# One set of statistics for two normalisations, and a reordered start, in an attention and MLP kernel

## The chip, the cores and the metric

The kernel is one program on one core of a Trainium2 chip. The metric is device time in microseconds (us), lower is better; the times given are those of single executions, and their median. The engines are TensorE (PE in the profile, PEld for its weight loads), VectorE (DVE), ScalarE (ACT), GpSimd (POOL) and SyncE (SP, which only issues transfers).

## The reference

```python
xn = layernorm(x)                      # x: (16, 512, 128), eps 1e-5
xn2 = layernorm(xn) * ln_g + ln_b      # inside the attention, a second time
q, k, v = (xn2 @ W + b for each)       # 16 heads of 8
content = (q + u_bias) @ k.T
pos = relative_shift((q + v_bias) @ (pe @ Wp).T)
attn = softmax((content + pos) / sqrt(8))
x = x + (attn @ v) @ Wo + bo + ffn(xn) # ffn: three layers of +-1 weights, relu between
```

All is float32. The relative shift moves row i of a head's 512x512 position scores by an amount that depends on i.

## The kernel before

**Batches, units and halves.** The kernel works through 16 batches. A batch has 16 heads; one head of one batch is a unit, and a unit has two halves, so a batch has 32 halves (h = 0 to 31 below, counted on over the batches). Each engine runs one loop over all halves and does its own share of each. TensorE computes position scores of a unit (L586, two 26x512 matmuls in most halves); ScalarE copies them to `pos_sb` (L394, L396); SyncE writes them to `shift` in HBM; ScalarE issues the load back with another pitch, which is the relative shift. It is issued 8 halves after the unit's first. Twelve halves after it, TensorE computes the content scores (L596), and VectorE adds the loaded position scores and takes the row extreme (L496), then subtracts it (L501). Seventeen halves after it, TensorE transposes the result (L605) into `ps_pt` and ScalarE takes the exponential (L404); TensorE multiplies with the values (L619).

**Jobs.** Everything else is a job, which TensorE does between these: T1 and TZ transpose the once and the twice normalised rows, QG, KG and PG (one for each of four groups of heads) compute queries, keys and the position table, V the values, L0, L1, L2 the layers of the MLP, TO, TH, WO, TY the output. Tuples `(half, name, group)` written out by hand (`START`, `FIRST`, `FIRST_NEXT`, `THIS`, `NEXT`, `LAST`) say in which half a job is done. All jobs write one PSUM bank, `ps_job`, and a job's first matmul waits until the job before has been copied out (L570, `wait(pe, s_jev, k - 1)`). ScalarE copies out all but V, TO, WO and TY, which VectorE takes (V at L441).

**Splits.** A matmul of full float32 precision is made of reduced ones: GpSimd splits what T1, L0, L1, QG, KG and PG gave into a high and a low part (`split`, L317 and L318 for the stacks `QS`, `KS`, `PS`; L326 and L327 for the MLP), from a ring of three buffers, `act_sb`.

**Normalisation.** `norm_stats(b, k)` on VectorE (L429, L432) takes mean and variance of `x` (k = 0) or of the once normalised `x1_sb` (k = 1), `norm(b, k)` on GpSimd raises the variance to the power -0.5 (L299, L300), and `scale_rows` (L237) writes `x1_sb` or `z_sb`; VectorE scales batch 0, GpSimd the others. Statistics for batch it + 2 stand in slots 6 and 8 of batch it (a slot is two halves), the scaling in slots 7 and 10. For batch 1 these slots fall before half 0, so each engine reaches them before its first half. The second statistics wait for the first scaling:

```python
else:
    dve.wait_ge(s_x1, b + 1)
```

**The start.** SyncE issues all loads. TensorE and ScalarE begin when all weights are there and VectorE has worked out three biases (`s_bias`, L469 to L475). Then come the jobs of `START` and the loop.

## Time and profile before

| | us |
|---|---|
| median of 3 runs | 1565.9 |
| lowest, highest | 1565.02, 1566.18 |
| the profiled execution | 1561.8 |
| its span, first to last instruction | 1560.0 |
| first position matmul (half 0) starts | 26.59 |
| half 12 (first content scores) starts | 62.89 |
| half 0 of batch 1 starts | 126.49 |
| one batch of the steady state | 92.5 |

Start times of halves are those of their first L586 matmul in the timeline. Busy shares over the span: TensorE 96%, VectorE 87%, ScalarE 80%, GpSimd 48%. DMA moves 353 GB/s in the mean; the highest of the page's 40 slices has 423. A row of the windows view has, after the stretch and its length in us, the busy time and number of instructions of PE, PEld, DVE, ACT and POOL, then the granted clock of TensorE, the DMA engines' busy share, and GB/s. A timeline row has start, duration, engine, line, operation, output<-input, sizes, and in brackets the idle time before it with what ended it. The page reads: busy time first, then the span in 40 slices, then the chain of work that ended last. A busy share is a mean over stages with different limits, so the stages have to be read one by one.

### The profile page before, as it was taken

What the parts mean: (1) busy time and instruction counts of PE and PEld (TensorE: products, weight loads), DVE (VectorE), ACT (ScalarE), POOL (GpSimd) and SP (SyncE); (2) the same over time, 40 slices, a digit from 0 to 9 for tenths busy, and PEclk for the clock granted to TensorE, in tenths of its full rate; (3) what the DMA queues carried; (4) which work ended last, traced back from release to release, by engine and by line L of the source; (5) the groups of instructions that cost most, each with busy time, mean ns of one, the idle gap of its engine ahead of it and who ended that gap; (6) DMA issues with size and microseconds to landing.
All of it is one profiled execution on the core that took longest, in us unless ns stands there. A gap on an engine that the chain in (4) does not pass through costs nothing.

```text
span 1560.0 us, 41383 instructions
## 1 busy us (share of the span) xinstructions
PE 1492.3 (96%) x16040; PEld 972.9 (62%) x16040; DVE 1350.5 (87%) x3593; ACT 1242.0 (80%) x1367; POOL 744.7 (48%) x743
## 2 busy tenths in 40 slices
PE   3989999999999999999999999999999999999997
PEld 1366666666666666666666666666666666666664
DVE  3278998989889898989989899898989989898895
ACT  1678888888888788878878888788888878887873
POOL 4864635445364554625455363554636455442300
PEclk9999999999999999999999999999999999999999
DMA  2799999999999999999999999999999999999992
GB/s 63 285 332 364 355 384 355 380 366 373 374 351 375 366 363 383 358 384 356 382 366 371 374 351 381 364 377 364 368 384 356 377 360 380 371 371 381 351 423 95
DMA packets 80435, 550.40 MB, mean 353 GB/s; under 512 B 9328, under 2 KB 10096, under 8 KB 14704
## 3 DMA queue, kind: packets, MB, share of 16 engines
q1 hardware_dynamic: 43376, 279.31, 48.2%
q10 hardware_dynamic: 36864, 268.45, 46.4%
q8 instruction: 128, 2.10, 0.5%
q14 instruction: 67, 0.55, 0.1%
HBM read 274.57 MB, written 273.15 MB: 351 GB/s over the span
## 4 chain that ended last, share of the span: by engine, by line
PE 72%; DVE 19%; issue 4%; ACT 4%; POOL 1%; DMA 0%; ACTq 0%; POOLq 0%; DVEq 0%
PE ps_pt L605 25%; PE ps_av L619 12%; PE ps_job L562 12%; PE ps_pos L586 10%; DVE sc_sb L496 8%; DVE sc_sb L501 7%; PE ps_job L523 4%; PE ps_job L526 3%; ACT pt_sb L404 3%; DVE stats L429 2%; PE ps_job L541 1%; PE ps_con L596 1%; PE ps_job L532 1%; PE ps_job L537 1%; DVE mv L432 1%
## 5 line engine op out<-in xcount | busy, mean ns | idle before, releaser
L496 DVE CUSTOM_DVE_ANT_0 sc_sb<-ps_con,sc_sb 128x512 f32<-128x512 f32 x1024 | 663.3, 684 | 155.2 <-PE ps_con L596 152.4
L394 ACT COPY pos_sb<-ps_pos 128x1024 f32<-128x1024 f32 x510 | 520.6, 1021 | 163.7 <-PE ps_pos L586 161.2
L501 DVE TENSOR_SCALAR sc_sb<-sc_sb,nmax 128x512 f32<-128x512 f32 x1024 | 604.7, 630 | 0.1
L605 PE MATMUL ps_pt<-c_sb,sc_sb 128*128 128x128 f32 x4096 | 560.4, 280 | 15.6 <-ACT pt_sb L404 8.5
L404 ACT ACTIVATE pt_sb<-ps_pt 128x1024 f32<-128x1024 f32 x512 | 526.4, 1028 | 45.5 <-PE ps_pt L605 44.9
L605 PEld LDWEIGHTS ps_pt<-c_sb,sc_sb 128*128 128x128 f32 x4096 | 441.6, 142 | 145.0 <-issue 79.9
L619 PE MATMUL ps_av<-pt_sb,v_sb 128*9 128x128 f32 x8192 | 320.7, 274 | 2.1 <-DVE o_sb L509 1.1
L619 PEld LDWEIGHTS ps_av<-pt_sb,v_sb 128*9 128x9 f32 x8192 | 173.0, 90 | 197.0 <-issue 192.9
L596 PE MATMUL ps_con<-k_stack,q_stack 26*128 26x512 f32 x1024 | 277.2, 497 | 14.6 <-DVE nmax L496 11.8
L586 PE MATMUL ps_pos<-p_stack,q_stack 26*128 26x512 f32 x1024 | 270.3, 504 | 0.8 <-POOLq L320 0.5
L326 POOL CAST h<-act_sb 128x512 fp32r<-128x512 f32 x128 | 80.3, 627 | 239.3 <-ACT act_sb L370 238.4
L317 POOL TENSOR_TENSOR q_stack<-act_sb,c_sb 128x512 fp32r<-128x512 f32 x64 | 66.9, 1046 | 240.1 <-ACT act_sb L367 239.7
L586 PEld LDWEIGHTS ps_pos<-p_stack,q_stack 26*128 26x128 f32 x1024 | 100.8, 184 | 127.2 <-issue 112.8
L562 PE MATMUL ps_job<-h,w 128*128 128x512 f32 x640 | 173.6, 410 | 0.6 <-ACT act_sb L370 0.3
L327 POOL TENSOR_TENSOR h<-act_sb,h 128x512 fp32r<-128x512 f32 x128 | 166.5, 1301 | 10.3
L317 POOL TENSOR_TENSOR k_stack<-act_sb,c_sb 128x512 fp32r<-128x512 f32 x64 | 67.4, 1053 | 170.1 <-ACT act_sb L367 169.9
L370 ACT ACTIVATE act_sb<-ps_job,col 128x512 f32<-128x512 f32 x128 | 88.8, 694 | 59.8 <-PE ps_job L562 59.7
L562 PEld LDWEIGHTS ps_job<-h,w 128*128 128x128 f32 x640 | 114.6, 191 | 24.4 <-DVE heads L449 3.7
L596 PEld LDWEIGHTS ps_con<-k_stack,q_stack 26*128 26x128 f32 x1024 | 104.2, 182 | 32.6 <-DVE nmax L496 30.6
L318 POOL TENSOR_TENSOR q_stack<-act_sb,q_stack 128x512 fp32r<-128x512 f32 x64 | 82.3, 1286 | 5.0
L318 POOL TENSOR_TENSOR k_stack<-act_sb,k_stack 128x512 fp32r<-128x512 f32 x64 | 82.1, 1283 | 5.0
L496 DVE DVE_READ_ACCUMULATOR2_ANT nmax<- 128x1 f32 x1024 | 83.4, 81 | 0.0
(70 smaller groups left out, 969.8 us busy)
## 6 DMA issues: line engine op xcount, KB each, us to landing
...
x_sb<-in_x SPq DMA_DIRECT2D x16, 256.0 KB, 9.5
out<-x_sb SPq DMA_DIRECT2D x16, 256.0 KB, 10.9
...
o_t<-in_wp SPq DMA_DIRECT2D x1, 256.0 KB, 5.7
heads<-in_pe_t SPq DMA_DIRECT2D x1, 256.0 KB, 6.9
```

What stands on the lines that cost most here:

```text
L317: own(pool.tensor_tensor(dst, src, low.broadcast_to([P, S]), ALU.mult))
L318: pool.tensor_tensor(dst, src, dst.bitcast(F32), ALU.subtract).then_inc(s_hl, 1)
L327: pool.tensor_tensor(dst[:, 1, :], src, dst[:, 0, :].bitcast(F32), ALU.subtract) \
L394: act.copy(to, ps_pos[:, :, :]).then_inc(s_pe, 1)
L404: act.activation(pt_sb[:, 2 * i:2 * i + 2, :], ps_pt[:, :, :], ACT.Exp, scale=-1.0) \
L496: dve.tensor_tensor_reduce(sc_sb[:, m % N_SC, t, :], ps_con[:, k, :], sc_sb[:, m % N_SC, t, :], -SCALE, 3.4e38, ALU.add, ALU.min, nmax[:, ...
L501: dve.tensor_scalar(sc_sb[:, m % N_SC, t, :], sc_sb[:, m % N_SC, t, :], nmax[:, m % N_SC, t:t + 1], None, ALU.subtract).then_inc(s_sub, 1)
L562: return pe.matmul(ps_job[:, :], lhs, src[:, a, hl, :], start=(a == 0 and hl == 0), stop=(a == len(before) - 1 and hl == 1))
L586: ins = pe.matmul(ps_pos[:, bank, :], QS[rows, g, t * P:(t + 1) * P], PS[rows, g, :], start=True, stop=True)
L596: pe.matmul(ps_con[:, bank, :], QS[rows, g, t * P:(t + 1) * P], KS[rows, g, :], start=True, stop=True).then_inc(s_con, 1)
L605: last = pe.transpose(ps_pt[:, j % 2, t * P:(t + 1) * P], sc_sb[:, u % N_SC, t, j * P:(j + 1) * P], id_sb)
L619: last = pe.matmul(ps_av[32 * t:32 * t + DH + 1, h % 4, :], v_sb[:, b % 2, j, h, :], pt_sb[:, j, t * P:(t + 1) * P], start=(j == 0), stop= ...
```

## The change

1. **One set of statistics.** The second normalisation scales `x` with the first one's mean, and its factor comes from the same variance v: (v (1 + eps) + eps^2)^-0.5 in place of the statistics of `x1_sb`. `norm_stats(b)` runs once for each batch (slot 6), `scales(b)` on GpSimd makes both factors at once: two small operations and one power over 8 columns. The scalings stay in slots 7 and 10.
2. **Batches 0 and 1.** VectorE takes the statistics of batch 1 in half 1 and does both its scalings in half 6, GpSimd its factors in half 2. Of batch 0, `z_sb` is scaled first, `x1_sb` later.
3. **Own banks.** The seven jobs of the new `START` (TZ, PG 0, QG 0, KG 0, PG 1, PG 2, PG 3) write banks of `ps_pt`, `ps_con` and `ps_job` that are not yet in use (`BANK`), and don't wait for the job before. QG, KG and PG among them are copied to free score buffers (`RAW`) instead of the ring. VectorE splits PG 0 to 3 and QG 0, GpSimd KG 0.
4. **Waits and loads.** ScalarE issues the loads of `consts`, `wp` and `pe`, SyncE the others. A small ScalarE activation at the start brings its table load forward. TensorE waits for `consts` alone before TZ, and for each bias where it is used; the bias for `wp` is made first.
5. **The order of batch 0's jobs.** PG 1, PG 2 and PG 3 leave halves 2, 5 and 11. V moves from half 0 to 2, L0 from halves 6, 8, 9, 10 to 4, 6, 8, 10, and L1 from 13, 14, 18, 19 to 12 to 15. Halves 18 and 19 have no job any more.

The names in the rows below: `z_sb` and `x1_sb` are the normalised rows (TZ, T1), `z_q` and `z_t` the transposed ones (QG; KG and V), `heads`/`o_t` hold the position encoding and its weights at the start (PG), `w0`, `w1`, `w2` the MLP weights. TensorE from its first matmul on, before:

```order
L549 MATMUL ps_job<-c_sb,z_sb 128x128 x4
L523 MATMUL ps_job<-z_q,stack_w_sb 128x512
L529 MATMUL ps_job<-heads,o_t 128x512
L526 MATMUL ps_job<-z_t,stack_w_sb 128x512
L586 MATMUL ps_pos<-p_stack,q_stack 128x512
L549 MATMUL ps_job<-c_sb,x1_sb 128x128 x4
L537 MATMUL ps_job<-c_sb,z_t 128x128 x4
L586 MATMUL ps_pos<-p_stack,q_stack 128x512
L523 MATMUL ps_job<-z_q,stack_w_sb 128x512
L586 MATMUL ps_pos<-p_stack,q_stack 128x512 x2
L529 MATMUL ps_job<-heads,o_t 128x512
```

and after:

```order
L613 MATMUL ps_pt<-c_sb,z_sb 128x128 x4
L593 MATMUL ps_con<-heads,o_t 128x512
L587 MATMUL ps_pt<-z_q,stack_w_sb 128x512
L590 MATMUL ps_job<-z_t,stack_w_sb 128x512
L593 MATMUL ps_con<-heads,o_t 128x512 x3
L662 MATMUL ps_pos<-p_stack,q_stack 128x512
L613 MATMUL ps_job<-c_sb,x1_sb 128x128 x4
L662 MATMUL ps_pos<-p_stack,q_stack 128x512
L587 MATMUL ps_job<-z_q,stack_w_sb 128x512
```

The PG matmuls now stand ahead of the first `ps_pos` matmul, and half 0 has lost V. VectorE between the MLP weights and its first values, before:

```order
L483 TENSOR_SCALAR w1<-pt_sb 128x2048
L484 TENSOR_SCALAR w2<-pt_sb 128x512
L429 BN_STATS stats<-x_sb 128x6 x4
L432 BN_AGGR mv<-stats 128x2 x4
L429 BN_STATS stats<-x1_sb 128x6 x4
L432 BN_AGGR mv<-stats 128x2 x4
L441 TENSOR_TENSOR v_sb<-ps_job,c_sb 128x64x8
```

and after, from the last split of the position table on:

```order
L482 TENSOR_TENSOR p_stack<-sc_sb,c_sb 128x512
L483 TENSOR_TENSOR p_stack<-sc_sb,p_stack 128x512
L538 TENSOR_SCALAR w0<-pt_sb 128x512
L539 TENSOR_SCALAR y_t<-pt_sb 128x512
L540 TENSOR_TENSOR w0<-w0,y_t 128x512
L541 TENSOR_SCALAR w1<-pt_sb 128x2048
L542 TENSOR_SCALAR w2<-pt_sb 128x512
L475 BN_STATS stats<-x_sb 128x6 x4
L478 BN_AGGR mv<-stats 128x2 x4
L491 TENSOR_TENSOR v_sb<-ps_job,c_sb 128x64x8
L251 TENSOR_SCALAR x1_sb<-x_sb,mv,rstd 128x128 x4
L251 TENSOR_SCALAR z_sb<-x_sb,mv,rstd 128x128 x4
```

The second statistics, which read what GpSimd scaled, are gone from the place ahead of `v_sb`, and the scaling of batch 1 stands behind it. The diff, cut to its core:

```diff
-        START = ((0, "TZ", 0), (1, "QG", 0), (2, "PG", 0), (3, "KG", 0))
...
+        START = ((0, "TZ", 0), (1, "PG", 0), (2, "QG", 0), (3, "KG", 0), (4, "PG", 1), (5, "PG", 2), (6, "PG", 3))
...
+        BANK = {("TZ", 0, 0): ps_pt[:, 0, :], ("QG", 0, 0): ps_pt[:, 1, :], ("PG", 0, 0): ps_con[:, 0, :],
+                ("PG", 0, 1): ps_con[:, 1, :], ("PG", 0, 2): ps_con[:, 0, :], ("PG", 0, 3): ps_con[:, 1, :],
+                ("KG", 0, 0): ps_job[:, :]}
...
-        STATS_SLOTS, NORM_SLOTS = (6, 8), (7, 10)
...
+            return [b if 0 <= b < B and slot == k else None for k in (6, 7, 10)]
...
+            def scales(b):
+                pool.wait_ge(s_st, b + 1)
+                own(pool.tensor_scalar(var_eps[:, 0, :], mv[:, :, 1], EPS, None, ALU.add))
+                own(pool.tensor_scalar(var_eps[:, 1, :], mv[:, :, 1], 1.0 + EPS, EPS * EPS, ALU.mult, ALU.add))
+                own(pool.tensor_tensor(rstd[:, :, :].rearrange("p k t -> p (k t)"),
+                                       var_eps[:, :, :].rearrange("p k t -> p (k t)"), half_pow[:, :], ALU.pow))
...
+                _, first, second = slot_of(h // 2)
+                if h % 2 == 0 and first is not None:
+                    scales(first)
+                    norm(first, 0)
+                if h % 2 == 0 and second is not None:
+                    norm(second, 1)
...
-            act.wait_ge(s_w, 64)
+            act.dma_start(c_sb[:, :], consts).then_inc(s_c, 16)
+            act.dma_start(wp_sb[:, :], wp).then_inc(s_w, 16)
+            act.dma_start(pe_sb[:, :], pe_t).then_inc(s_w, 16)
             act.wait_ge(s_ones, ONES)
...
+            norm_stats(0)
+            dve.wait_ge(s_rstd, 1)
+            scale_rows(dve, 0, 1)
+            dve.wait_ge(s_c, 16)
+            dve.wait_ge(s_w, 48)
...
+            dve.wait_ge(s_jev, job("PG", 0, 0))
+            stack(PS[:, 0, :], RAW[("PG", 0, 0)], LOW_K, s_ps)
+            dve.wait_ge(s_jev, job("QG", 0, 0))
+            stack(QS[:, 0, :], RAW[("QG", 0, 0)], LOW_Q, s_qs)
+            scale_rows(dve, 0, 0)
+            for c in range(1, GROUPS):
+                dve.wait_ge(s_jev, job("PG", 0, c))
+                stack(PS[:, c, :], RAW[("PG", 0, c)], LOW_K, s_ps)
...
+                if h == 1:
+                    norm_stats(1)
+                if h == 6:
+                    dve.wait_ge(s_rstd, 2)
+                    dve.wait_ge(s_job, job("T1", 0))
+                    scale_rows(dve, 1, 0)
+                    scale_rows(dve, 1, 1)
...
+                if part == 0 and (name, b, c) in BANK:
+                    if name in ("QG", "PG") and c < 2:
+                        pe.wait_ge(s_w, 48)
+                    if name == "PG":
+                        pe.wait_ge(s_bias, 1)
+                        if c >= 2:
+                            pe.wait_ge(s_jev, job("PG", 0, c - 2))
+                    if name == "QG":
+                        pe.wait_ge(s_jev, job("TZ", 0))
+                    if name == "KG":
+                        pe.wait_ge(s_bias, 2)
+                        pe.wait_ge(s_zt, 1)
```

ScalarE copies out `z_q` right after TZ, then PG 0, then QG 0, and only then makes `z_t`, which sets `s_zt`.

## Rows read from the trace of the kernel before

**Rows 1.** Windows of batch 0's first 20 halves: busy time of each engine, clock, DMA.
```profile
26.59:37.98 11.39, 6.61 (x16) 3.53 (x17) 1.83 (x9) 1.95 (x4) 9.05 (x12) 1.00 0.00 0
37.98:62.89 24.91, 24.48 (x42) 7.86 (x42) 0.00 (x0) 16.80 (x20) 23.07 (x23) 1.00 0.56 211
62.89:74.84 11.95, 11.23 (x35) 5.67 (x35) 7.92 (x25) 6.53 (x8) 9.57 (x11) 1.00 1.02 381
74.84:92.62 17.78, 14.27 (x97) 9.65 (x96) 11.76 (x34) 11.18 (x13) 12.06 (x13) 0.90 0.82 321
```

**Rows 2.** The same view for two whole batches of the steady state.
```profile
404.28:498.20 93.92, 92.21 (x1006) 60.95 (x1003) 84.34 (x223) 77.20 (x86) 46.47 (x46) 0.98 0.99 363
498.20:590.70 92.50, 90.73 (x1006) 59.88 (x1003) 84.19 (x223) 77.20 (x86) 46.68 (x46) 1.00 1.00 368
```

**Rows 3.** Windows: half 14 and halves 16 to 21, batch 6, then batch 14.
```profile
631.79:635.58 3.79, 2.99 (x33) 1.74 (x29) 3.75 (x16) 2.04 (x3) 2.97 (x4) 1.00 1.00 409
638.71:655.28 16.57, 16.27 (x188) 10.50 (x184) 15.96 (x46) 15.63 (x19) 10.99 (x11) 1.00 1.01 344
1373.53:1376.15 2.62, 2.51 (x33) 1.57 (x29) 2.62 (x9) 2.05 (x3) 0.00 (x0) 1.00 0.98 397
1379.28:1395.82 16.54, 15.81 (x189) 10.32 (x185) 15.83 (x38) 15.59 (x19) 8.74 (x8) 1.00 1.02 391
```

**Rows 4.** Waits, 26 to 36 us: engine and line waited for; total, times, longest.
```profile
DVE stats L429 <- POOL x_sb L237: 16.0, 1, 16.0
...
PE ps_job L523 <- DVE v_sb L441: 4.1, 1, 4.1
```

**Rows 5.** The same view, 76 to 90 us.
```profile
DVE stats L429 <- POOL x_sb L237: 2.2, 1, 2.2
```

**Rows 6.** Timeline from the start: start us, us, engine, line, work [idle before].
```profile
3.83 0.87 DVE L429 BATCH_NORM_STATS2 stats<-x_sb 128x6 f32<-128x128 f32 x4 [2.44 <-DMA x_sb<-in_x]
...
5.53 1.04 POOL L300 TENSOR_TENSOR rstd<-var_eps,half_pow 128x4 f32<-128x4 f32 x1
...
10.62 1.11 DVE L237 TENSOR_SCALAR z_sb<-x_sb,mv,rstd 128x128 f32<-128x128 f32 x4 [1.53 <-POOLq L302]
...
12.46 0.28 DVE L469 TENSOR_TENSOR biased<-o_t,c_sb 128x128 f32<-128x128 f32 x1
...
13.92 1.08 PE L549 MATMUL ps_job<-c_sb,z_sb 128*128 128x128 f32 x4 [13.92 <-DVE col L476]
...
15.11 1.28 ACT L361 ACT_TABLE_LOAD   x1 [15.11 <-PE ps_job L549]
...
17.08 1.25 ACT L362 ACTIVATE z_t<-ps_job,c_sb 128x512 f32<-128x512 f32 x1
...
20.50 0.69 ACT L367 ACTIVATE act_sb<-ps_job,c_sb 128x512 f32<-128x512 f32 x1 [2.17 <-PE ps_job L523]
...
21.23 2.08 PE L529 MATMUL ps_job<-heads,o_t 128*128 128x512 f32 x2 [0.78 <-ACT act_sb L367]
```

**Rows 7.** DMA issues: size, microseconds from issue to landing.
```profile
heads<-in_pe_t SPq DMA_DIRECT2D x1, 256.0 KB, 6.9
```

**Rows 8.** Timeline of later halves of batch 0, TensorE and GpSimd.
```profile
44.43 2.07 PE L523 MATMUL ps_job<-z_q,stack_w_sb 128*128 128x512 f32 x2
44.45 1.04 POOL L317 TENSOR_TENSOR p_stack<-act_sb,c_sb 128x512 fp32r<-128x512 f32 x1 [0.18 <-ACT act_sb L367]
...
47.00 1.04 POOL L317 TENSOR_TENSOR k_stack<-act_sb,c_sb 128x512 fp32r<-128x512 f32 x1 [0.18 <-POOL p_stack L318]
...
56.88 1.22 PE L562 MATMUL ps_job<-x_t,w 128*128 128x512 f32 x2
```

**Rows 9.** Timeline, where the matmuls get faster.
```profile
66.48 3.63 PE L562 MATMUL ps_job<-h,w 128*128 128x512 f32 x8
...
70.89 2.12 PE L562 MATMUL ps_job<-h,w 128*128 128x512 f32 x8 [0.34 <-ACT act_sb L370]
...
73.78 1.12 PE L526 MATMUL ps_job<-z_t,stack_w_sb 128*128 128x512 f32 x2 [0.34 <-ACT act_sb L370]
```

More of the change, by code:

```diff
@@ L124, in attention_mlp @@
         ps_job = psum("ps_job", [P, S])
+        s_c = sem("s_c")
         s_w = sem("s_w")
@@ L310, in split @@
                 pool.wait_ge(s_jev, job(name, b, c))
-                if name in ("QG", "KG", "PG"):
-                    dst, low, ready = {"QG": (QS, LOW_Q, s_qs), "KG": (KS, LOW_K, s_ks),
-                                       "PG": (PS, LOW_K, s_ps)}[name]
+                if name in ("QG", "KG"):
+                    dst, low, ready = {"QG": (QS, LOW_Q, s_qs), "KG": (KS, LOW_K, s_ks)}[name]
                     dst = dst[:, c, :]
+                    if b == 0 and c == 1 and name == "QG":
+                        pool.wait_ge(s_qs, 1)
                     if b > 0:
@@ L534, in block @@
                     def block(t):
-                        dst, cut = ps_job[:, t * P:(t + 1) * P], slice(t * P, (t + 1) * P)
+                        dst, cut = out[:, t * P:(t + 1) * P], slice(t * P, (t + 1) * P)
                         if name == "V":
```

141 lines of the change are left out of this document (79 added, 62 removed).

## The prediction, made before the changed kernel was run

> **What bounds the kernel now.** I read the chain of waits first: it lies mostly on TensorE, then on VectorE. Such a share mixes stages, so next come the start times of the halves in the timeline, and then the windows and the waits of the stretches that stick out.
>
> The steady state repeats itself to a few hundredths: a batch takes 92.5 us, and two batches take 1.42 longer (93.92); in those the granted clock is 0.98 in place of 1.00 [rows 2]. Batch 0 is different. From the first position matmul (26.59) to batch 1 it takes 99.9 (126.49 - 26.59), 7.4 more than a steady one, and 26.59 go by before it. Three things stand out. Its halves 0 and 1 take 11.39, with TensorE busy for 6.61 of them [rows 1]. VectorE waits there 16.0 us for GpSimd's scaling of batch 1, because the second statistics need it; V of batch 0 stands behind that wait, `ps_job` stays full, and TensorE waits 4.1 [rows 4]. Later, in halves 16 to 19 (17.78 for work of which TensorE does 14.27), VectorE waits 2.2 for the same reason, behind GpSimd's queue of splits, and the clock is at 0.90 [rows 1, 5]. Third, the start: TZ begins only at 13.92, when VectorE has finished the last bias, though `z_sb` was ready at 11.7 [rows 6].
>
> **Statistics, in the steady state: nothing.** The change takes one block of about 1.2 us off VectorE in each batch. VectorE is busy 84 of 92.5 us, so it looks as if this could give 1.2 in each of 14 batches. The trace has its own test of this: batch 14 has neither block, since no batch 16 follows. The first block (slot 6) costs TensorE 3.79 - 2.62 = 1.17 us in half 14; this block stays. Around the second (slot 8), halves 16 to 21 take 16.57 with it and 16.54 without, since ScalarE is busy for 15.6 of them either way [rows 3]. So I take 0.0 for the block that goes, between 0 and a gain of 0.03 a batch. On GpSimd slot 10 loses a small operation and a power of about 1.04, slot 7 gains one small operation and four more columns of power. No row shows a power over 8 columns. The one over 4 takes 1.04, as long as a product over 512 [rows 6, 8], so the price hardly goes by columns; bounds are 0 and another 1.04. I take 0, and the upper bound is a rival below.
>
> **The start: 2.1 us earlier.** x has landed at 3.83, the power starts at 5.53 and takes 1.04 [rows 6]. One more small GpSimd step costs less than the power; estimate 0.3. So the scaling of `z_sb` (1.11) starts at 5.53 + 0.3 + 1.13 = 7.0 in place of 10.62 and ends at 8.1. TZ (1.08) follows, to 9.3; the 1.28 of the table load has left the path, since ScalarE does it while it waits for x [rows 6]. PG 0 needs the position table's loads and the first bias. The last of these loads took 6.9 us from issue [rows 7]; issued third on ScalarE, 1 to 3 us in, it lands at 8 to 10. The bias took at most 1.5 (12.46 to 13.92, with what follows it) [rows 6]. PG 0 starts between 9.3 and 10.8; I take 9.9. Then PG 0 and QG 0, 2.08 each, to 14.1. Now a wait that the change adds: ScalarE copies QG 0 (0.7) before it makes `z_t` (1.25), and KG 0 waits for `z_t`, with PG 1 to 3 queued behind it on TensorE: 16.1. Four matmul jobs of 2.08 without a pause give 24.4, and the first position matmul starts at 24.5 in place of 26.59. **Term: -2.1**, bounds -2.7 and -1.1. VectorE's splits of PG 0 and QG 0 are done by 17, well before; GpSimd's of KG 0 is needed only in half 12.
>
> On the loads, the trace shows that SyncE issues them one after the other and that the last lands 6.9 after its issue. The Trainium skill (DMA: Bandwidth & Descriptors, Issuing engines are not separate DMA queues) says that two issuing engines share the same 16 DMA engines, and that only the time of issuing is saved. By that rule the split of the issues alone gives about an issue or two, and x can land a little later since it now shares the engines with `consts`; with PG 0 at 10.8 the term would be -1.2.
>
> **Halves 0 to 11: 6.5 us less.** Now 11.39 + 24.91 = 36.30 [rows 1]. A half with QG, KG or PG takes its matmuls, 2.07, and 0.78 until ScalarE has emptied the bank: 2.85. One with L0 takes 1.22 + 0.78 = 2.0 [rows 6, 8]. After: half 0 with T1 alone 1.8, half 1 (QG) 2.8, half 2 (V) 2.9, five with KG or QG 14.25, four with L0 8.0, sum 29.8. **Term: -6.5.** V now waits for VectorE's MLP weights and the statistics of batch 1, which end at about 31 while V's matmuls end at 32; the cover is 1 us, and beyond it each us costs one. GpSimd has 6 stacks of 2.55 (44.45 to 47.00) [rows 8], 5 other splits of about 2 and the factors of batch 1 (1.7): 27.0 in 29.8 us. It just keeps up. Bounds: -6.9 and -5.
>
> **Halves 12 to 15: 1.7 us more.** Now 11.95 [rows 1]. They get all four L1. One costs 3.63 + 0.78 = 4.4 where the matmuls speed up in its midst, 2.12 + 0.78 = 2.9 after it [rows 9]. 4.4 + 3 x 2.9 = 13.1; if the clock rises one half later, 14.4. I take 13.7. **Term: +1.7**, bounds +1.2 and +2.4.
>
> **Halves 16 to 19: 8.0 us less.** Now 17.78 [rows 1]. L1 2 and 3 are gone from 18 and 19, VectorE's wait (2.2) [rows 5] is gone, and with it the fall of the clock that followed TensorE's stall. What remains is TZ's two copies and the ordinary work: per half, VectorE and ScalarE have about 2.4, with TZ near 2.8. 9.8 together, bounds 9.2 and 11.6. **Term: -8.0**, bounds -8.6 and -6.2. What is late next is GpSimd: its scaling of batch 2 waits for T1 of batch 1, which is in half 16, with the split of L1 3 and of T1 queued behind. I have that split done 1.5 us before L0 of half 20 asks for it.
>
> The other twelve halves keep their jobs, and so do all batches from 1 on: 0.
>
> **The sum.** -2.1 - 6.5 + 1.7 - 8.0 = -14.9. Against the profiled execution that is a span of 1560.0 - 14.9 = 1545.1 and a time of 1561.8 - 14.9 = 1546.9. The median of the runs is 4.1 above the profiled execution, and the start of a program doesn't depend on that, so from the median: 1565.9 - 14.9 = **1551.0**. The bounds of the terms add up to -18.2 and -9.9; two or none of the clock's falls in the steady state, or two more, shift it by 2.8 either way. The likeliest case alone: 1547 to 1555.
>
> **Rivals.**
>
> *The clock rises in the start.* The matmuls of L1 get from 3.63 to 2.12 for eight, those of a stack from 2.07 to 1.12 [rows 8, 9], though the granted clock reads 1.00 throughout [rows 1]: these are the two levels, 1.2 and 2.4 GHz. It rose inside eight matmuls without a pause, not in the 25 us of alternating position matmuls and jobs before. The new start has 8.3 us of jobs without a pause. If they raise it, PG 2 and 3 give 2.1, halves 0 to 11 fall to GpSimd's 27.0 (2.8 less), and L1 0 gives 1.5: 6.4 more, 1544.6. Against it: the matmuls of QG and PG filled some 70% of those 25 us and raised nothing. The Trainium skill (TensorE: Matmul & The Clock Gate, What's actually happening) says that the low rate is the default and that activity releases it, which would speak for this rival.
>
> *Part of the gain is given back in batch 0.* Two mechanisms: GpSimd's queue at half 20 runs out of its 1.5 us, or V waits for VectorE; or the transfers bind, since halves of 2.4 ask for 2 x 1.05 MB in 4.8 us, 437 GB/s, where halves 12 to 15 moved 381 [rows 1]. Each gives back 2 to 5 us, together up to 6: 1555 to 1557.
>
> *Slower: GpSimd's slot 7.* If the power over 8 columns costs another 1.04 and the small step 0.3, the split of QG 3, which waits behind the scaling, comes late in each of 14 batches, the ring fills and ScalarE and TensorE wait. At 1.34 a batch that is 18.8 us against 14.9: 1554.9 if half of it shows, 1569.8 if all. It decides from 1.1 us a batch on. Against it: GpSimd is busy for only 46.7 of 92.5 us [rows 2].
>
> *The change doesn't do what it says*, because a new wait keeps TensorE from starting before 26 and halves 18 and 19 stay long: a gain under 3.1, 1564.
>
> **Chances.** The forecast 0.56, the early clock 0.18, given back 0.19, no difference 0.03, slower 0.04. The range takes in the early clock and nearly all of the given-back case: 1543.5 to 1557.5. About 0.2%, 3.1 us, is what a measurement can tell here: faster 0.93, same 0.03, slower 0.04.
>
> **What would show it.** TZ at 8 to 9 us; the first position matmul at 24.5 (26 or more: the start's term is wrong); half 12 at 54.3; batch 1 at 111.6 in place of 126.49; a batch of 92.5 as before, with half 14 still at 3.8; TensorE's matmuls of 2.07 until half 12. The prediction is wrong if batches become shorter than 92.3 (then the second statistics did cost something) or longer than 92.7 (GpSimd), or if halves 0 to 11 take more than 32.

## The result, and the profile after

The changed kernel takes 1550.3 us in the median of 4 runs (1547.8 to 1553.57), the kernel before beside it 1566.04 (1565.02 to 1566.75). The ratio is 0.9901, with a 95% interval of 0.9879 to 0.9923: faster by 1.0%. The prediction was 1551.0, so the number is right. The working behind it is right only in part: two of its steps failed in opposite directions.

The page of the profiled execution (1551.94 us), its first line and the 40 slices of granted clock:

```profile
span 1550.1 us, 41206 instructions
...
PEclk8799999999999999999999999999999999999999
```

In the clock row the second slice (39 to 78 us) is at 0.7. The windows view over the first 20 halves answers [rows 1]: halves 0 and 1, 2 to 11, 12 to 15, 16 to 19. The fifth row is half 3 alone, the sixth halves 4 to 11, the last a batch of the steady state, for [rows 2].

```profile
21.39:24.52 3.13, 2.64 (x9) 1.08 (x9) 3.10 (x4) 2.15 (x4) 1.66 (x3) 1.00 0.00 0
24.52:55.01 30.49, 23.05 (x47) 8.12 (x46) 12.62 (x24) 16.21 (x19) 22.82 (x22) 0.58 0.51 180
55.01:68.30 13.29, 12.40 (x49) 7.73 (x48) 8.83 (x25) 6.63 (x8) 8.88 (x9) 0.81 0.97 363
68.30:78.91 10.61, 8.27 (x83) 5.39 (x82) 10.00 (x26) 9.58 (x11) 9.77 (x11) 0.91 1.01 381
26.46:35.60 9.14, 2.50 (x5) 0.68 (x5) 6.97 (x16) 1.01 (x1) 4.50 (x5) 0.66 0.29 116
35.60:55.01 19.41, 18.96 (x33) 6.28 (x32) 3.74 (x8) 13.60 (x16) 16.38 (x16) 0.50 0.66 228
112.82:205.46 92.64, 90.40 (x1006) 59.66 (x1002) 84.14 (x215) 77.23 (x86) 46.22 (x45) 1.00 1.00 365
```

The two long halves of the kernel before are gone (11.39 became 3.13). In their place stands half 3 with 9.14 us, in which TensorE works for 2.50. From then to half 12 its clock is at 0.50.

| | before | predicted | after |
|---|---|---|---|
| first position matmul (half 0) | 26.59 | 24.5 | 21.39 |
| halves 0 to 11 take | 36.30 | 29.8 | 33.62 |
| half 12 starts | 62.89 | 54.3 | 55.01 |
| halves 12 to 15 take | 11.95 | 13.7 | 13.29 |
| halves 16 to 19 take | 17.78 | 9.8 | 10.61 |
| half 0 of batch 1 starts | 126.49 | 111.6 | 112.82 |
| most batches of the steady state | 92.5 | 92.5 | 92.62 |

Of the gain 13.67 us are there when batch 1 begins. Batches 1 to 14 give back 0.7, the last batch 1.5 and what follows it 1.6; the spans differ by 9.9 (1560.0 to 1550.1). The last batch and what follows it vary between executions of the same code: they take 88.66 and 50.7 here, 86.66 to 87.94 and 49.1 to 51.9 in the experiment kernels, 87.16 and 49.1 before. The single profiled executions stand differently to their medians, 4.2 below it before and 1.6 above it after. That is why the medians differ by 15.7. How much of the 5.8 beyond the spans' 9.9 is the change's stays open.

**The start.** The timeline of the changed kernel up to half 0, for [rows 6]:

```profile
4.64 0.87 DVE L475 BATCH_NORM_STATS2 stats<-x_sb 128x6 f32<-128x128 f32 x4 [3.25 <-DMA x_sb<-in_x]
...
6.62 1.67 POOL L313 TENSOR_TENSOR rstd<-var_eps,half_pow 128x8 f32<-128x8 f32 x1
...
9.63 1.09 PE L613 MATMUL ps_pt<-c_sb,z_sb 128*128 128x128 f32 x4 [9.63 <-DVE z_sb L251]
...
10.51 1.98 PE L593 MATMUL ps_con<-heads,o_t 128*128 128x512 f32 x2
...
16.23 2.04 PE L590 MATMUL ps_job<-z_t,stack_w_sb 128*128 128x512 f32 x2 [2.03 <-ACT z_t L396]
...
18.06 3.39 PE L593 MATMUL ps_con<-heads,o_t 128*128 128x512 f32 x6
...
21.39 0.50 PE L662 MATMUL ps_pos<-p_stack,q_stack 26*128 26x512 f32 x1
```

TZ starts 1.4 us later than forecast: x is there 0.81 later, and the power over 8 columns takes 0.63 more. KG 0 still starts at 16.23 (forecast 16.1). PG 0 follows right behind TZ at 10.51, 0.6 after the forecast 9.9, and it and QG 0 take 3.7 together in place of 4.2. An earlier TZ would have helped little: in e8 below, with TZ 1.05 earlier, PG 0 starts 0.35 earlier and waits for its bias. Then comes the surprise: six PG matmuls take 3.39 in place of 6.2, and the first position matmul has 0.50 where it has 0.79 at the low rate. TensorE has gone to 2.4 GHz in these matmuls, near 19 us; in the kernel before it did so in the last of the eight matmuls from 66.48 on [rows 9], some 50 us later. (Ahead of the first rise the views give a granted clock of 1.00, though the matmuls run at the low rate, so the start is read from the matmuls.)

**Half 3.** Waits of the changed kernel between 24 and 36 us, for [rows 4], and VectorE's timeline there:

```profile
ACT act_sb L414 <- PE ps_job L590: 7.7, 1, 7.7
...
PE ps_job L590 <- DVE v_sb L491: 6.6, 1, 6.6
```

```profile
25.01 1.64 DVE L483 TENSOR_TENSOR p_stack<-sc_sb,p_stack 128x512 fp32r<-128x512 f32 x1
26.58 1.26 DVE L538 TENSOR_SCALAR w<-pt_sb 128x512 fp32r<-128x512 uint8 x1
27.76 1.48 DVE L539 TENSOR_SCALAR y_t<-pt_sb 128x512 f32<-128x512 uint8 x1
29.27 0.69 DVE L540 TENSOR_TENSOR w<-w,y_t 128x512 fp32r<-128x512 f32 x1
29.88 1.22 DVE L541 TENSOR_SCALAR w<-pt_sb 128x2048 fp32r<-128x2048 uint8 x1
...
31.68 0.87 DVE L475 BATCH_NORM_STATS2 stats<-x_sb 128x6 f32<-128x128 f32 x4 [0.25 <-DVE w L542]
32.59 0.38 DVE L478 BATCH_NORM_AGGREGATE mv<-stats 128x2 f32<-128x6 f32 x4
32.88 0.66 DVE L491 TENSOR_TENSOR v_sb<-ps_job,c_sb 128x512 f32<-128x512 f32 x1
```

V's matmuls end at 26.5, and VectorE empties their bank at 32.88, after its MLP weights and statistics. TensorE stands idle for 6.6 us, more than the 5.2 that it gained in the start, and after that its clock is low again.

### The profile page after: what moved, and what is told of

Its sections match the earlier page's. It is cut to its first block, busy times and chain, and to the rows that moved or that the text cites. A ratio compares the mean times of both kernels' runs of the same rounds, so it can differ in the third digit from the quotient of the medians.

```text
span 1550.1 us, 41206 instructions
## 1 busy us (share of the span) xinstructions
PE 1483.5 (96%) x16040; PEld 968.8 (62%) x16040; DVE 1360.5 (88%) x3483; ACT 1241.5 (80%) x1368; POOL 722.2 (47%) x709
## 4 chain that ended last, share of the span: by engine, by line
PE 75%; DVE 14%; ACT 5%; issue 3%; DMA 3%; ACTq 0%; POOL 0%; DVEq 0%; POOLq 0%
PE ps_pt L681 26%; PE ps_av L695 13%; PE ps_job L626 12%; PE ps_pos L662 10%; DVE sc_sb L559 5%; DVE sc_sb L564 5%; PE ps_job L590 4%; PE ps_job L587 4%; ACT pt_sb L453 3%; DMA sc_sb<-shift 2%; ACT z_t L409 1%; PE ps_con L672 1%; PE ps_job L605 1%; PE ps_job L596 1%; DVE stats L475 1%
## 5 line engine op out<-in xcount | busy, mean ns | idle before, releaser
L564 DVE TENSOR_SCALAR sc_sb<-sc_sb,nmax 128x512 f32<-128x512 f32 x1024 | 617.5, 643 | 0.1
L672 PE MATMUL ps_con<-k_stack,q_stack 26*128 26x512 f32 x1024 | 273.0, 497 | 12.2 <-DVE nmax L559 10.3
L346 POOL TENSOR_TENSOR h<-act_sb,h 128x512 fp32r<-128x512 f32 x128 | 170.4, 1331 | 10.3
```

The lines of the kernel that those rows point to most:

```text
L346: pool.tensor_tensor(dst[:, 1, :], src, dst[:, 0, :].bitcast(F32), ALU.subtract) \
L564: dve.tensor_scalar(sc_sb[:, m % N_SC, t, :], sc_sb[:, m % N_SC, t, :], nmax[:, m % N_SC, t:t + 1], None, ALU.subtract).then_inc(s_sub, 1)
L672: pe.matmul(ps_con[:, bank, :], QS[rows, g, t * P:(t + 1) * P], KS[rows, g, :], start=True, stop=True).then_inc(s_con, 1)
```

## The experiments

Each kernel ran beside the kernel before on the same chip. That one took 1566.04 us beside the changed kernel, but 1562.35 to 1564.25 beside the others, so times are to be compared by the last column; the expectations below speak of times for 1566. The table gives the starts of halves in the profiled executions, and the runs' times. In each of these executions two to four of the batches 1 to 14 take 93.8 to 94.0 us in place of 92.6, at a lower granted clock (the first of [rows 2] is one), so a difference of 1 or 2 us between two kernels says little.

| kernel | half 0 | half 12 | half 20 | batch 1 | median (lowest to highest) | ratio to before (95%) |
|---|---|---|---|---|---|---|
| before | 26.59 | 62.89 | 92.62 | 126.49 | | |
| changed | 21.39 | 55.01 | 78.91 | 112.82 | 1550.3 (1547.8 to 1553.57) | 0.9901 (0.9879 to 0.9923) |
| e1_stats_alone | 24.66 | 57.95 | 83.69 | 116.87 | 1553.31 (1551.66 to 1554.59) | 0.9926 (0.9910 to 0.9943) |
| e2_second_block | 21.48 | 54.08 | 76.92 | 110.83 | 1550.38 (1548.14 to 1551.28) | 0.9908 (0.9893 to 0.9923) |
| e3_v_first | 21.10 | 47.26 | 73.00 | 106.87 | 1543.93 (1540.92 to 1546.0) | 0.9867 (0.9852 to 0.9882) |
| e4_one_bank | 28.97 | 59.76 | 82.40 | 115.80 | 1554.84 (1553.83 to 1556.24) | 0.9939 (0.9924 to 0.9954) |
| e5_sync_loads | 20.14 | 54.03 | 77.12 | 110.51 | 1549.1 (1547.29 to 1552.4) | 0.9915 (0.9897 to 0.9934) |
| e6_more_splits | 21.41 | 42.54 | 67.64 | 101.00 | 1542.94 (1537.62 to 1545.94) | 0.9873 (0.9842 to 0.9904) |
| e7_gpsimd_splits | 22.75 | 51.94 | 74.93 | 108.34 | 1548.63 (1546.53 to 1550.14) | 0.9909 (0.9892 to 0.9925) |
| e8_power4 | 22.39 | 54.95 | 77.94 | 111.29 | 1548.41 (1546.63 to 1549.32) | 0.9900 (0.9878 to 0.9921) |
| e9_v_first_again | 21.34 | 47.46 | 73.22 | 107.03 | 1541.69 (1538.62 to 1542.47) | 0.9852 (0.9825 to 0.9878) |
| e10_more_splits_again | 21.45 | 42.56 | 67.69 | 101.08 | 1539.71 (1538.21 to 1544.5) | 0.9851 (0.9825 to 0.9876) |
| e11_all | 21.59 | 42.67 | 69.16 | 103.54 | 1541.81 (1541.11 to 1543.6) | 0.9861 (0.9839 to 0.9882) |
| e12_two_powers | 23.43 | 55.76 | 79.96 | 115.53 | 1551.0 (1549.03 to 1556.47) | 0.9909 (0.9875 to 0.9943) |

### e1_stats_alone: one part of the change by itself

The kernel before, with one set of statistics and nothing else of the change:

```diff
-        STATS_SLOTS, NORM_SLOTS = (6, 8), (7, 10)
+        STATS_SLOTS, NORM_SLOTS = (6,), (7, 10)
...
-                if k == 0:
-                    dve.wait_ge(s_x[b % N_X], 16 * (b // N_X + 1))
...
-                else:
-                    dve.wait_ge(s_x1, b + 1)
```

> The kernel before with one set of statistics and nothing else of the change: the jobs, banks, splits and loads are those of before. Theory: the statistics are most of the gain, since both waits of VectorE for GpSimd's scaling go with them, and the second one's wait also took the clock down. Start: the second statistics and power leave VectorE's path, 1.9 us less, the first position matmul near 24.7. Half 1 falls from 6.91 to about 2.9, halves 18 and 19 from 13.0 to about 6.5. Sum 12 less: 1554. Rival: only the two waits seen in the waits view are won, 4.1 + 2.2, so 1559.7. A steady batch should be 92.5 by both.

Batch 1 begins at 116.87, which is 9.6 of the 13.7 us. Half 1 falls from 6.91 to 2.86, and V no longer waits for GpSimd. The time is the theory's: 0.9926 of 1566 is 1554.5, forecast 1554. Windows of halves 0 and 1, and of 16 to 19:

```profile
24.66:32.01 7.35, 6.61 (x17) 3.54 (x17) 0.69 (x1) 1.96 (x4) 6.52 (x8) 1.00 0.00 0
...
69.72:83.69 13.97, 12.69 (x98) 8.34 (x98) 11.20 (x28) 10.93 (x13) 13.12 (x14) 1.00 1.01 396
```

Read beside [rows 1] (11.39 and 17.78), these rows show what the wait cost: 4.0 us in halves 0 and 1 (the first row), where TensorE's work is the same 6.61, and 3.8 in halves 16 to 19. There TensorE is busy for 12.69 in place of 14.27, because the clock, 0.90 before, stays up: part of the 3.8 is the clock that the stall had taken. Another 1.9 are in the start, where second statistics and a second power no longer stand between the scalings of `x1_sb` and `z_sb`. Seven tenths of the change's gain at batch 1 come from the single set of statistics, not from the starts that its diff spends most lines on.

### e2_second_block: the removed work, put back without its dependence

The changed kernel, and VectorE takes a second, unused set of statistics of `x` in slot 8:

```diff
+                    for t in range(NT):
+                        last = dve.bn_stats(stats_b[:, t, :], x_sb[:, extra % N_X][:, t, :])
+                    own(last)
+                    for t in range(NT):
+                        last = dve.bn_aggr(mv_b[:, t, :], stats_b[:, t, :])
```

> The changed kernel with a second block of statistics put back on VectorE in slot 8 of each batch, as long as the one removed (1.25 us), from x and unused, so that it waits for nothing. Theory: ScalarE bounds halves 16 to 21, the block costs nothing in the steady state: a batch stays at 92.6 and the time at 1550 (within 2). Rival: VectorE's 1.25 us count in each of 14 batches: a batch of 93.8, 1567.

```profile
110.83:203.43 92.60, 90.71 (x1008) 60.04 (x1004) 84.29 (x223) 77.26 (x86) 45.99 (x45) 1.00 0.99 364
```

VectorE has its 223 instructions again as in [rows 2], and the batch takes 92.60 as without them. The work itself was all but free, as the prediction read from [rows 3]. The batch hides two differences of 0.1, though. Half 21 takes 2.95 to 2.97 in batches 1 to 13, which have the block, and 2.85 in batch 14, which has none; in the changed kernel it takes 2.86. And halves 2, 5, 8 and 10, which have the L1 jobs, take 15.71 together as before and 15.81 in the changed kernel. The L1 job of half 10 of batch 3, before, changed and here:

```profile
343.26 2.07 PE L562 MATMUL ps_job<-h,w 128*128 128x512 f32 x8
...
329.78 2.12 PE L626 MATMUL ps_job<-h,w 128*128 128x512 f32 x8
...
327.68 2.07 PE L636 MATMUL ps_job<-h,w 128*128 128x512 f32 x8
```

The block stands only in slot 8 of batches 0 to 13. So this run shows that in halves 16 to 19 e1's gain is the dependence. In halves 0 and 1 the waits [rows 4] say the same, and the 1.9 of the start are work on the path, which this run doesn't put back.

### e3_v_first: what V's wait costs

```diff
-            dve.wait_ge(s_wb, 48)
-            half0 = y_t[:, :]
...
-                if h == 1:
-                    norm_stats(1)
...
+                if h == 2:
+                    first_weights()
+                    norm_stats(1)
+                    other_weights()
```

VectorE now takes V out before it makes the MLP weights and the statistics of batch 1 (GpSimd's factors move from half 2 to 4).

> The changed kernel with V of batch 0 taken by VectorE ahead of the MLP weights and of the statistics of batch 1, which follow it in half 2 (GpSimd's factors then in half 4). In the changed kernel TensorE waits 6.6 us for V's copy in half 3. Theory: the early position matmuls (21.4) only ran into that wait, and it is VectorE's queue that holds half 12 at 55.0. With V first, half 3 falls from 9.14 to below 3.5 and half 12 comes at 49 to 51, so about 5 less: 1545.5. Rival: L0 of half 4, which needs the MLP weights, inherits the wait; then half 4 grows by 3 or more and the gain is 1 to 2: 1549.

```profile
26.28 0.69 DVE L491 TENSOR_TENSOR v_sb<-ps_job,c_sb 128x512 f32<-128x512 f32 x1 [1.63 <-PE ps_job L606]
```

```profile
27.03 1.12 PE L595 MATMUL ps_job<-z_t,stack_w_sb 128*128 128x512 f32 x2 [0.35 <-DVE v_sb L491]
...
40.40 2.07 PE L592 MATMUL ps_job<-z_q,stack_w_sb 128*128 128x512 f32 x2 [2.52 <-ACT act_sb L419]
```

Half 3 takes 1.91 in place of 9.14, half 12 starts 7.8 us earlier, and the time falls to 0.9867 of before, 5 us better than the changed kernel. Beyond its 6.6 us the wait had cost the clock: without it the stacks run at 1.12 us a pair until half 8, and halves 4 to 8 take 9.3 in place of 11.7. Then the next limit shows, the waits of e3 between 40 and 48 us:

```profile
PE ps_job L592 <- ACT act_sb L419: 2.5, 1, 2.5
ACT act_sb L419 <- POOL q_stack L337: 2.3, 1, 2.3
```

ScalarE finds no free buffer in the ring because GpSimd is behind, TensorE stands for 2.5 us, and the clock falls again (2.07 for the pair). Half 9 takes 5.02 in place of 2.85, so nearly all that the clock had given is gone again.

### e4_one_bank: the start's jobs in one bank

```diff
-        BANK = {("TZ", 0, 0): ps_pt[:, 0, :], ("QG", 0, 0): ps_pt[:, 1, :], ("PG", 0, 0): ps_con[:, 0, :],
+        BANK = {j: ps_job[:, :] for j in (("TZ", 0, 0), ("QG", 0, 0), ("PG", 0, 0), ("PG", 0, 1), ("PG", 0, 2),
...
-                if part == 0 and (name, b, c) not in BANK:
+                if part == 0:
```

> The changed kernel with all seven jobs of the start in the one bank of before, each waiting until the job before has been copied out; order, splits and loads stay. Theory: each job then takes 2.85 in place of 2.08, z_t is made before PG 0, the first position matmul starts at 29 to 30 and not at 21.4; the jobs are no longer without a pause, so the matmuls stay at 2.08 and don't speed up before half 12. Of the 8 us the wait for V eats most: half 12 comes at 59 to 60 in place of 55.0, 1554.8. Rival: the start counts in full, 8 more: 1558.5.

```profile
21.47 2.08 PE L591 MATMUL ps_job<-heads,o_t 128*128 128x512 f32 x2 [0.78 <-ACT sc_sb L395]
...
26.96 2.07 PE L591 MATMUL ps_job<-heads,o_t 128*128 128x512 f32 x2 [0.67 <-ACT sc_sb L390]
28.97 0.79 PE L655 MATMUL ps_pos<-p_stack,q_stack 26*128 26x512 f32 x1
```

With 0.7 us of pause between them the jobs stay at the low rate, and half 0 starts 7.6 us later. Yet batch 1 starts only 3.0 us later than in the changed kernel (5.0 later than in e2): V's matmuls now end when VectorE is nearly ready (half 3 takes 3.99). So 2.6 to 4.6 of the 7.6 us that own banks gain in the start have ended in V's wait or behind it by then. The median is the forecast 1554.8 as it stands; by its ratio it is 1556.5, between the theory's 1554.8 and the rival's 1558.5, and the interval is too wide (2.4 us either way) to choose. Halves and batch 1 speak for the theory.

### e5_sync_loads: the loads from one engine

```diff
+            sp.dma_start(c_sb[:, :], consts).then_inc(s_c, 16)
...
-            act.dma_start(c_sb[:, :], consts).then_inc(s_c, 16)
-            act.dma_start(wp_sb[:, :], wp).then_inc(s_w, 16)
-            act.dma_start(pe_sb[:, :], pe_t).then_inc(s_w, 16)
```

> The changed kernel, but SyncE issues all loads again, in the old order (x, consts, the stacked weights, wp, pe, then the rest). It prices the loads from two engines alone. In the changed kernel x_sb is there at 4.64 us, 0.81 later than before (3.83), and PG 0 starts at 10.51 right behind its predecessors. Theory: x arrives alone again, near 3.85, so TZ starts about 0.8 earlier than 9.63; but pe and wp are issued behind three other loads and PG 0 waits for them until 11 to 12, so half 0 starts at 21.4 to 22.4 in place of 21.39, and the median is 1550.3 to 1551.3, nothing that can be told from the changed kernel. Rival: the issuing engine matters more than that, and the last load that PG 0 needs lands at 13 or later; then half 0 starts at 24 or later and the time is 1553 or more.

```profile
8.85 1.09 PE L613 MATMUL ps_pt<-c_sb,z_sb 128*128 128x128 f32 x4 [8.85 <-DVE z_sb L251]
...
10.60 2.05 PE L593 MATMUL ps_con<-heads,o_t 128*128 128x512 f32 x2 [0.66 <-DVE o_t L522]
...
16.39 1.10 PE L590 MATMUL ps_job<-z_t,stack_w_sb 128*128 128x512 f32 x2 [2.04 <-ACT z_t L396]
17.32 2.88 PE L593 MATMUL ps_con<-heads,o_t 128*128 128x512 f32 x6
```

x lands 0.79 earlier, the position table's loads later, and PG 0 starts at 10.60 in place of 10.51: issuing from two engines is worth 0.1 us here. In e8 below, where PG 0 waits for its bias as it does here, two engines have it start at 10.16, 0.44 earlier. Half 0 nonetheless starts 1.25 earlier, which I had not expected: the clock rose already for KG 0 (1.10). The times can't be told from those of the changed kernel. The Trainium skill (DMA: Bandwidth & Descriptors, Issuing engines are not separate DMA queues) says that only time of issuing is saved; this trace agrees, by 0.1 us (0.44 against e8's, where the last of these loads is issued 1.4 us earlier).

### e6_more_splits: GpSimd relieved

e3_v_first, and VectorE also splits QG 2 and QG 3 of batch 0:

```diff
+                    if j in (("QG", 0, 2), ("QG", 0, 3)):
+                        dve.wait_ge(s_jev, job(*j))
+                        dve.wait_ge(s_qs, j[2])
+                        stack(QS[:, j[2], :], RAW[j], LOW_Q, s_qs)
```

> The kernel of e3_v_first, and VectorE also splits QG 2 and QG 3 of batch 0, which takes two of GpSimd's stacks (2.55 us each) off its queue. In e3 half 9 took 5.02 us, since ScalarE waited 2.3 for a free buffer of GpSimd's ring, TensorE stood idle for 2.5 and its clock fell again, so that L1 0 and L1 1 took 4.72 and 4.56. Theory: GpSimd is the next limit there; without those two stacks half 9 takes 2.0 to 2.9, the clock stays up, half 12 starts at 43 to 45 in place of 47.26, L1 takes 2.9, half 16 starts at 55 to 58 in place of 62.38, and the time is 1538 to 1541. Rival: the transfers bind (halves of 2.0 to 2.4 us ask for 1.05 MB each 2 of them, over 430 GB/s, where the page never shows more than 423): then halves 12 to 16 wait for sc_sb from the DMA, half 20 starts within 1 us of e3's 106.87 - 33.9 = 73.0, and the time is 1543 to 1545.

```profile
21.41:42.54 21.13, 16.85 (x55) 6.58 (x54) 16.97 (x26) 17.67 (x23) 16.72 (x16) 1.00 0.52 188
42.54:57.83 15.29, 12.63 (x47) 7.49 (x46) 13.45 (x31) 6.58 (x8) 12.79 (x12) 0.89 1.02 394
```

Half 9 takes 1.64 in place of 5.02, halves 0 to 11 take 21.13 us at a granted clock of 1.00, and half 12 starts at 42.54. The transfers don't bind: half 20 starts at 67.64, where the rival had 73.0. What is late next is L1 0 (half 12 takes 5.00): its matmuls wait for GpSimd's splits of L0, 1.62 us in the longest case, and the clock falls once more. Batch 1 starts 5.9 us before e3's, but the time misses the forecast of 1538 to 1541: 0.9873 of 1566 is 1546, no better than e3's 0.9867. The two were on different chips; e9 and e10 ask again.

### e7_gpsimd_splits: VectorE's splits undone

```diff
-                    if (name, b, c) == ("KG", 0, 0):
-                        pool.wait_ge(s_jev, job("KG", 0))
-                        stack(KS[:, 0, :], RAW[("KG", 0, 0)], LOW_K, s_ks)
+                    if (name, b, c) in RAW:
...
+                        stack(dst[:, c, :], RAW[(name, b, c)], low, ready)
```

> The changed kernel, but GpSimd does all six of the start's splits; VectorE's five (PG 0 to 3, QG 0) go to it, in the order of the jobs. It is the part 'VectorE splits five of them' undone alone. Five stacks of 2.55 us are 12.8 us more on GpSimd. Theory: the first position matmul, which needs PG 0 and QG 0, moves little (its TensorE work ends at 21.4 anyway), V no longer waits 6.6 us for VectorE (its matmuls' bank is emptied at 27 to 28), but GpSimd runs behind from half 1 on: QG 1's split comes at 31 or later and ScalarE waits for the ring; half 12 starts at 56 to 60 in place of 55.01 and the time is 1552 to 1556. Rival: GpSimd catches up while TensorE is at its low rate, and with V's wait gone half 12 starts at 49 to 52; then the time is 1545 to 1548 and the split on VectorE was of no use.

```profile
28.67 1.13 PE L585 MATMUL ps_job<-z_t,stack_w_sb 128*128 128x512 f32 x2 [0.35 <-DVE v_sb L493]
...
32.19 1.06 PE L621 MATMUL ps_job<-x_t,w 128*128 128x512 f32 x2 [1.96 <-POOL x_t L346]
```

V's wait is gone and halves 4 and 7 wait for GpSimd in its place (3.45 and 4.20 in place of 2.00 and 2.86). Half 12 starts at 51.94, as the rival had it (49 to 52). Batch 1 starts at 108.34, 4.5 us before the changed kernel's, of which two more slow batches take 3.0 back in this execution. The time is the changed kernel's (0.9909; of 1566 that is 1552, at the lower end of my forecast of 1552 to 1556, not the rival's 1545 to 1548). In this form of the start, moving five stacks to VectorE moved the queue rather than shortening it.

This kernel also prices an overlap. VectorE's first weights run here while GpSimd is idle, the later ones beside its split:

```profile
12.42 0.42 DVE L533 TENSOR_SCALAR w<-pt_sb 128x512 fp32r<-128x512 uint8 x1
...
13.27 1.53 POOL L321 TENSOR_TENSOR p_stack<-sc_sb,c_sb 128x512 fp32r<-128x512 f32 x1 [4.98 <-ACT sc_sb L390]
13.82 2.06 DVE L536 TENSOR_SCALAR w<-pt_sb 128x2048 fp32r<-128x2048 uint8 x1
14.88 2.15 POOL L322 TENSOR_TENSOR p_stack<-sc_sb,p_stack 128x512 fp32r<-128x512 f32 x1
15.81 1.51 DVE L537 TENSOR_SCALAR w<-pt_sb 128x512 fp32r<-128x512 uint8 x1
```

The same 128x512 conversion takes 0.42 alone and 1.51 beside GpSimd, and GpSimd's split 1.53 and 2.15 where it takes 1.04 and 1.28 alone. The Trainium skill (SBUF — State Buffer, Who interferes with whom) says that a `tensor_scalar` in a two-port mode takes a port pair that VectorE shares with GpSimd, that whoever comes second stands still for it, and that a `tensor_tensor` with two SBUF inputs contends with GpSimd's reads. The rows fit: both sides get longer, and in the changed kernel a `p_stack` operation takes 1.64 in place of 0.69. In which mode this conversion runs they don't show.

### e8_power4: the first power over four columns

```diff
+            own(pool.tensor_scalar(var_eps[:, 1, :], mv[:, :, 1], 1.0 + EPS, EPS * EPS, ALU.mult, ALU.add))
+            own(pool.tensor_tensor(rstd[:, 1, :], var_eps[:, 1, :], half_pow[:, 0:NT], ALU.pow))
+            pool.sem_inc(s_rstd, 1)
```

> The changed kernel, but for batch 0 GpSimd works out the factor of the second normalisation first and alone: one small operation and a power over 4 columns, and the other factor behind it. In the changed kernel the power over 8 columns takes 1.67 us, the one over 4 in the kernel before took 1.04. Theory: the power's price goes up with its columns, 1.04 here again (0.16 per column beyond some 0.4), and with the small operation of 0.32 that leaves the path TZ starts at 8.65 to 8.7 in place of 9.63. PG 0 then waits for its bias or its loads and starts at 9.6 to 10.1 in place of 10.51; half 0 starts at 20.5 to 21.0 in place of 21.39. V's wait in half 3 grows by what the start gained, since VectorE's queue sets its end, so half 12 moves by less than 0.5 and the time is 1549.5 to 1550.3, not to be told from the changed kernel. Rival: the 1.67 is what any power takes behind two operations of GpSimd's in a row; then TZ is at 9.3 and nothing else moves.

```profile
6.19 1.04 POOL L351 TENSOR_TENSOR rstd<-var_eps,half_pow 128x4 f32<-128x4 f32 x1
...
8.58 1.09 PE L619 MATMUL ps_pt<-c_sb,z_sb 128*128 128x128 f32 x4 [8.58 <-DVE z_sb L251]
...
10.16 2.05 PE L599 MATMUL ps_con<-heads,o_t 128*128 128x512 f32 x2 [0.49 <-DVE o_t L527]
...
17.77 4.69 PE L599 MATMUL ps_con<-heads,o_t 128*128 128x512 f32 x6
```

The power's price goes with its columns (1.04 for 4, 1.67 for 8), and TZ starts where expected. PG 0 gains 0.35, and half 0 starts 1.0 *later*: the same six matmuls take 4.69, because the clock rose later in them. An earlier start was paid back by the clock. The time is that of the changed kernel.

### e9_v_first_again and e10_more_splits_again: the two side by side

> The kernel of e3_v_first once more, in one call with e10 and e11, because the two were timed on different chips so far (ratios 0.9867 and 0.9873). Theory: e10's batch 0 ends 5.9 us earlier (half 0 of batch 1 at 101.0, here at 106.87) and about 5 of it must be in the time: this kernel at 0.9867, e10 at 0.9830 to 0.9845 of the kernel before. Rival: the clock gives it back; executions of e10 that are not profiled fall to the low rate for longer (their mean clocks were 0.983, 0.986 and 0.996 beside 0.991 in the profiled one, the times 1545.2, 1545.9 and 1537.6), and then the two are within 1.5 us of each other, each with a wide spread that goes with the clock.

> The kernel of e6_more_splits once more. Theory: 1537.6 to 1541 in most executions, the one at 1545 an exception. Rival: its executions fall into two groups by the clock, near 1538 at a mean clock of 0.996 and near 1545 at 0.985, because in some of them the clock falls again in batch 0 and stays low for a long stretch; then the median is about 1542.5.

The profiled executions repeat to 0.2 us (batch 1 at 107.03 and 101.08). Spans are 1540.6 and 1536.4, so 4.2 of the 5.9 us are still there at the end; the rest lies in what follows the last batch, 49.1 against 50.8. But the medians are 1541.69 and 1539.71, and the ratios 0.9852 and 0.9851, each with 0.25% either way. So e9's theory, 5 us in the time, failed, and the ratios are its rival's. Of e10's own two, the theory held: three of four executions lie at 1538.2 to 1540.3 and one at 1544.5, and not in the rival's two groups by clock. The executions with the lower clock are the longer ones on the whole (e10: 1538.21 at 0.993, 1544.5 at 0.990), not without exception (1540.25 at 0.990). How much of e6's 5.9 us an execution keeps is open; both kernels beat the one before and the changed one.

### e11_all: e6, e5 and e8 together

> All that helped, together: e6_more_splits, the loads from SyncE in the old order (in e5_sync_loads half 0 started at 20.14 in place of 21.39), and the first power over 4 columns (e8_power4). Theory: TZ starts at 7.9, half 0 at 19.8 to 20.3, half 12 at 41 to 42, half 0 of batch 1 at 99 to 100, and the time is 1 to 2 us under e10. Rival: in some executions the clock falls in batch 0 and takes back more than that; then it can't be told from e10.

```profile
17.22 4.43 PE L611 MATMUL ps_con<-heads,o_t 128*128 128x512 f32 x6
```

TZ starts at 7.90 as expected, but PG 0 waits for its loads (10.67), and the clock rises for KG 0 (1.10 us) and is low again within the next six matmuls: half 0 at 21.59 (forecast 19.8 to 20.3). L1 of halves 13 and 14 then runs longer at the low rate (4.93 and 3.56 in place of e10's 4.48 and 2.91), and batch 1 starts 2.5 later than in e10. The rival held: nothing over e10.

### e12_two_powers: what slot 7's longer power costs

```diff
-                    scales(first)
...
+                    own(pool.tensor_tensor(rstd[:, 0, :], var_eps[:, 0, :], half_pow[:, 0:NT], ALU.pow))
                     norm(first, 0)
                 if h % 2 == 0 and second is not None:
...
+                    own(pool.tensor_tensor(rstd[:, 1, :], var_eps[:, 1, :], half_pow[:, 0:NT], ALU.pow))
                     norm(second, 1)
```

> The changed kernel, but from batch 2 on GpSimd works out each factor ahead of its own scaling (a power over 4 columns in slot 7 and one in slot 10, as in the kernel before, still from one set of statistics). It asks what the power over 8 columns in slot 7 costs the steady batches: in the changed kernel they take 92.62 us in place of 92.51, in half 0.03 pieces in halves 2, 5, 8 and 10. Theory: slot 7's extra power (0.63 us and a small operation of 0.3) ends in GpSimd's slack (it waits 1.4 us there before, 0.24 after), so a batch stays at 92.62 and the time within 1 us of the changed kernel's; the 0.11 comes from elsewhere. Rival: the longer slot 7 is what costs 0.11; then batches are 92.51 again and the time is 1.5 us lower.

```profile
208.40:301.00 92.60, 90.35 (x1004) 59.62 (x1003) 84.04 (x216) 77.18 (x86) 46.57 (x46) 1.00 1.00 372
```

Batches take 92.62 as in the changed kernel, so the power isn't what costs them 0.1 us. Every kernel with the single set alone, e1 too, has the 15.81 us in the four halves with L1, and e2 alone has the 15.71 of before. But e2 puts back the work of the second block and also its two tiles in SBUF, so it doesn't tell VectorE's load from where the tiles lie. Which of them it is stays open. In this execution the clock rose late in the start (PG 1 to 3 took 4.88) and half 0 came at 23.43.

## Why the prediction was right, and where it was not

**Steady state, 0: right.** e2 shows the removed block to cost 0.1 of its 1.25 us, in half 21, more than the bound of 0.03, and in the changed kernel as much is lost in the L1 jobs. In the kernel before half 21 takes 2.96 in only five of the 14 batches; batch 6, which [rows 3] show, is not one of them. So batches 1 to 14 are 0.7 us longer together in the profiled execution, 0.05 each, less than a measurement can tell. The rival of a slower slot 7 is out: the power did cost 0.63 more in the start and 0.45 in slot 7 (1.67 for 1.22), and GpSimd's slack took it (e12).

**The start, -2.1, measured -5.2.** KG 0 starts at 16.23 for a forecast 16.1, but by steps that were off and cancelled: x is there 0.81 later and the power is mis-sized by 0.63 (I took 0 between 0 and 1.04), which puts TZ at 9.63, outside the 8 to 9 that I had named as its sign; PG 0 starts only 0.6 late, since 9.9 had left room for its bias, and PG 0 and QG 0 together take 0.5 less than two times 2.08. With four jobs of 2.08 half 0 would be at 24.5, exactly as forecast. The jobs took 5.16 in place of 8.3 because the clock rose. That is the rival to which I gave 0.18, and e4 confirms its condition: with pauses of 0.7 us between the same jobs it doesn't rise. I had argued against it from QG and PG matmuls that filled some 70% of their time. That leaves out the position matmuls between them: TensorE was busy for 24.48 of those 24.91 us [rows 1]. So those 25 us tell of jobs that alternate with position matmuls, and e4 of jobs with pauses; neither has the jobs directly behind one another, as the new start has.

**Halves 0 to 11, -6.5, measured -2.7.** They take 33.62, and more than 32 was a sign that I had named for the prediction being wrong. It is, in this term. The step that failed is the cover of V's wait: "the cover is 1 us, and beyond it each us costs one". V's matmuls ended at 26.5, not at 32 (the clock and half 0 earlier), and VectorE reached V at 32.88, not at 31. The first is worth 5.5 us, the second 1.9; less the cover of 1 that is 6.4, and the wait was 6.6. VectorE was late, by my working of the 31, because I took its weights at the 0.42 of a time when GpSimd was idle; beside GpSimd's splits they took 1.26 and 1.48, a stack operation 1.64 for 0.69. And I had priced such a wait at its own length; e3 shows that it costs the clock for the 19 us behind it too: removing 6.6 us of wait brought half 12 forward by 7.8 (0.3 of it in the start), although in e3 GpSimd's stall of 2.5 took the clock away a second time. "TensorE's matmuls of 2.07 until half 12" failed as a sign both ways: a stack takes 1.12 between 19 and 29 us.

**Halves 12 to 15, +1.7, measured +1.3: right.** One L1 at the low rate (half 12 takes 4.56) and three at 2.9, as worked out. (With two at the low rate the terms give 14.6, not 14.4.)

**Halves 16 to 19, -8.0, measured -7.2: right within its bounds.** Its own terms, three halves of 2.4 and one of 2.8, add up to 10.0, not 9.8. The difference, 0.8, is in half 19 (3.36): the matmuls go to the low rate at 77 for a short time. In e5 to e8 half 19 takes 2.56 and the clock doesn't fall there.

**The number.** Two rivals came true together and cancelled: the early clock gave 3.1 us in the start, and halves 0 to 11 lost 3.8, which is V's wait of 6.6 less 2.8 that the early clock gave in the same halves. Without the wait, e3's 0.9867 is 1545, close to the early clock's 1544.6. Thus 1551.0 stands in the right place by a sum whose second term is wrong by more than half of itself. A second piece of luck is in the measure: 13.7 us are gained by batch 1, 9.9 at the end of the profiled executions, and 15.7 between the medians, for a forecast of 14.9. The ratio itself stands: the variants that time can't tell from the changed kernel have 0.9900 to 0.9915 (e2, e5, e7, e8, e12). Two sums of the prediction are off without having decided anything: the lower bounds of its terms add up to -17.0 (-17.4 with 0.03 a batch), not -18.2, and half of a slot 7 that costs 18.8 gives 1560.4, not 1554.9.
